# Second-layer work of two batches spread over four slots, and Gelu tiles in pairs, in a two-layer token tower

## The reference

```python
h = h + _L0_ffn_ref(_layernorm(h), ...)    # 8 heads, product keys, causal attention
h = h + _L1_attn_ref(_layernorm(h), Wq, Wk)   # q, k = x Wq^T, x Wk^T; softmax(q k^T / 8) @ x, no mask
h = h + _L1_ffn_ref(_layernorm(h), ...)    # experts, below

logits = tokens @ router_w.T; probs = softmax(logits)
rw, re = top_k(probs, 2); rw = rw / rw.sum(-1)
combine = zeros((N, 8)).at[arange(N)[:, None], re].set(rw)
out = tokens
for e in range(8):
    out = out + combine[:, e:e+1] * (gelu(tokens @ w1[e] + b1[e]) @ w2[e] + b2[e])
```

## Time and profile before

| | before |
|---|---|
| median of 3 runs | 3322.91 us (3321.53 to 3324.5) |
| the profiled execution's own time | 3329.95 us |
| its span | 3328.1 us |
| PE busy | 2803.7 us, 84% |
| VectorE busy | 2745.1 us, 82% |
| ScalarE busy | 2051.7 us, 62% |
| GpSimd busy | 2049.2 us, 62% |
| mean granted TensorE clock | 0.92 |

### The profile page before, as it was taken

How to read it: one execution, slowest core, us unless ns; L and a number is a source line. 1 busy time by engine, 2 the same in 40 slices (tenths; PEclk the granted TensorE clock), 3 DMA queues, 4 the chain that set the end, 5 groups by cost and what they waited for, 6 DMA issues and landing times. The chain is left out here.

```text
span 3328.1 us, 39343 instructions
## 1 busy us (share of the span) xinstructions
PE 2803.7 (84%) x9750; PEld 1333.8 (40%) x9750; DVE 2745.1 (82%) x10000; ACT 2051.7 (62%) x4514; POOL 2049.2 (62%) x2094
## 2 busy tenths in 40 slices
PE   4863466888989898989897989999988889899988
PEld 2431222343434343434344434344444434444433
DVE  8666987989898989897889998997989898966423
ACT  4222455676767676767686767676686767676422
POOL 4010577777777777777666777776657777776200
PEclk8975677999999999999898989999999899999989
DMA  1001122222222222222121222221212222221000
GB/s 43 26 10 49 34 65 63 64 64 61 67 64 65 63 64 65 63 64 63 49 67 41 70 61 70 56 73 50 66 47 62 65 65 63 64 63 49 20 0 4
DMA packets 85770, 179.92 MB, mean 54 GB/s; under 512 B 40193, under 2 KB 41251, under 8 KB 85542
## 3 DMA queue, kind: packets, MB, share of 16 engines
q0 software_dynamic: 66560, 135.40, 16.0%
q1 hardware_dynamic: 18982, 42.01, 4.0%
HBM read 176.22 MB, written 1.05 MB: 53 GB/s over the span
## 5 line engine op out<-in xcount | busy, mean ns | idle before, releaser
L1333 POOL DMA_INDIRECT mx_G<-in_kv_table,mx_slot_i x2048 | 1993.1, 973 | 815.4 <-issue 606.4
L1361 PE MATMUL mx_acc<-mx_W,mx_table 128*128 128x512 f32 x2048 | 1114.1, 626 | 0.3 <-ACT mx_kvT L1562 0.3
L1719 DVE SCALAR_TENSOR_TENSOR mx_W<-mx_D,mx_W 128x512 f32<-128x512 f32 x1024 | 697.2, 681 | 260.6 <-ACT mx_W L1555 258.5
L1623 ACT ACTIVATE mx_GT<-mx_G,mx_slot_w 128x128 f32<-128x128 f32 x2048 | 759.0, 494 | 208.9 <-DMA mx_G<-in_kv_table,mx_slot_i 208.5
L1555 ACT ACTIVATE mx_W<-mx_D 128x512 f32<-128x512 f32 x1024 | 606.9, 593 | 165.1 <-PE mx_D L1351 160.7
L1361 PEld LDWEIGHTS mx_acc<-mx_W,mx_table 128*128 128x128 f32 x2048 | 412.6, 203 | 193.8 <-issue 114.8
L1351 PE MATMUL mx_D<-mx_U,mx_pick_b 96*128 96x512 bf16 x1024 | 412.3, 403 | 60.0 <-DVE mx_W L1719 58.4
L1579 ACT ACTIVATE mx_PT<-mx_area 128x512 f32<-128x512 f32 x480 | 246.8, 514 | 284.9 <-PE mx_area L1411 147.0
L1373 PE MATMUL mx_O<-mx_PT,mx_KVs 128*65 128x512 f32 (+3 forms) x768 | 312.7, 489 | 16.9 <-ACT mx_OT L1571 8.7
L1387 PE MATMUL mx_area<-mx_KTa,mx_QTa 64*128 64x512 f32 (+3 forms) x384 | 179.3, 548 | 156.7 <-DVE mx_mx_part L1954 126.2
L1936 DVE TENSOR_REDUCE mx_KVs<-mx_GT 128x128 f32<-128x2048 f32 x128 | 291.8, 2280 | 6.9 <-ACT mx_GT L1623 6.7
(11 more groups left out here) (380 smaller groups left out, 4370.6 us busy)
## 6 DMA issues: line engine op xcount, KB each, us to landing
mx_table<-in_kv_dense SPq DMA_DIRECT2D x64, 512.0 KB, 3.7
mx_G<-in_kv_table,mx_slot_i POOLq DMA_INDIRECT x2048
tz_table<-in_c_dft SPq DMA_DIRECT2D x1, 2048.0 KB
tz_table<-in_c_idft SPq DMA_DIRECT2D x8, 256.0 KB, 2.6
out_h<-mx_xc SPq DMA_DIRECT2D x4, 256.0 KB, 3.8
mx_G<-in_c_pick SPq DMA_DIRECT2D x1, 528.0 KB
st_h<-in_tok_W,em_ids POOLq DMA_INDIRECT x32, 2.5
st_keys<-in_pk_keys SPq DMA_DIRECT2D x1, 512.0 KB, 3.9
```

The costliest lines, as they stand in the source:

```text
L1333: pool.indirect_dma_start(G[g % RING][:, r, :], None, a["kv_table"], bass.IndirectOffsetOnAxis(slot_i[n % 2][:, k, r:r + 1], 0))\
L1361: pe.matmul(acc[:, :], table[:, tile, :], W[c % TILE_RING][:, :], start=(tile == 0), stop=(tile == TILES - 1)).then_inc(applied, 1)
L1623: last = act.activation(GT[:, :, i], G[g % RING][:, i, :], ACT.Copy, scale=slot_w[n % 2][:, k, i:i + 1])
L1719: dve.scalar_tensor_tensor(W[c % TILE_RING][:, :], D_ps[c % 3][:, :], 0.0, W[c % TILE_RING][:, :], ALU.is_ge, ALU.mult).then_inc(w_done, 1)
```

## The change

Batches 0 and 1 get a fifth slot, which is slot s = 0 of the batch behind them: L1T tiles 0 to 7 stay in s = 2 and tiles 8 to 15 go to s = 3, at their positions 8 to 15; the second `l1y`, the norm, the router and the routing go from s = 2 to s = 3 at their positions; the experts, the final addition go from s = 3 to s = 4. Batches 2 and 3 stay as they were (`route_slot` is 2 there). For all batches the first norm goes from positions 11, 13, 14 to 22, 24, 25, and HID tiles come in pairs, at k = 1 and k = 3 of their half, none at k = 0 and 2. No operation is added or taken away in the source.

```diff
@@ area_uses @@
-    if p < 16 and 0 <= t - 6 < 4 * B:
-        b, s = divmod(t - 6, 4)
-        if s == 1:
-            return (("L1S", b, 0, p),)
-        if s == 2:
-            return (("L1T", b, 0, p),)
-        if s == 3:
-            return (("HID", b, p // 8, p % 8) if p % 8 < 4 else ("MY", b, 0, p // 8 * 4 + p % 8 - 4),)
+    if p < 16:
+        for b, s in cycle_of(t):
+            if s == 1:
+                return (("L1S", b, 0, p),)
+            if s == (2 if p < 8 else route_slot(b)):
+                return (("L1T", b, 0, p),)
+            if s == route_slot(b) + 1:
+                return expert_uses(b, p)
     return ()
+
+def route_slot(b):
+    return 3 if b < B - 2 else 2
+
+def expert_uses(b, p):
+    half, k = divmod(p, 8)
+    if k in (1, 3):
+        return (("HID", b, half, k - 1), ("HID", b, half, k))
+    return (("MY", b, 0, 4 * half + k - 4),) if k >= 4 else ()
+
+def cycle_of(t):
+    b, s = divmod(t - 6, 4)
+    stages = [(b - 1, 4)] if s == 0 and 0 < b <= B and route_slot(b - 1) == 3 else []
+    return stages + ([(b, s)] if 0 <= b < B else [])
@@ extra_uses @@
         if s == 2:
-            uses += [(10, ("l1y", b, 0)), (19, ("l1y", b, 1)), (28, ("l2x", b, 0)), (29, ("l2x", b, 1)), (32, ("l2r", b))]
+            uses += [(10, ("l1y", b, 0))]
+        if s == route_slot(b):
+            uses += [(19, ("l1y", b, 1)), (28, ("l2x", b, 0)), (29, ("l2x", b, 1)), (32, ("l2r", b))]
@@ tensor: the loop over q @@
-                elif uses:
-                    fill_area(uses[0])
+                else:
+                    for use in uses:
+                        fill_area(use)
@@ scalar: F @@
-                if (s, p) in ((0, 13), (2, 24)):
-                    act.wait_ge(ln_var, 2 * b + s // 2 + 1)
+                if p == 24 and s in (0, route_slot(b)):
+                    act.wait_ge(ln_var, 2 * b + (s > 0) + 1)
...
-                if (s, p) == (2, 35):
+                if (s, p) == (route_slot(b), 35):
@@ vector: F @@
-                n = s // 2
-                if (s, p) == (0, 11) and b:
+                n = int(s > 0)
+                if (s, p) == (0, 22) and b:
                     dve.wait_ge(out_stored, 16 * b)
-                if (s, p) in ((0, 11), (2, 22)):
+                if p == 22 and s in (0, route_slot(b)):
...
-                if (s, p) in ((0, 14), (2, 25)):
+                if p == 25 and s in (0, route_slot(b)):
...
-                if (s, p) == (2, 33):
+                if (s, p) == (route_slot(b), 33):
...
-                if (s, p) == (3, 17):
+                if (s, p) == (route_slot(b) + 1, 17):
@@ scalar and vector: the loop over q @@
-                if 0 <= t - 6 < 4 * B:
-                    F((t - 6) // 4, (t - 6) % 4, p)
+                for b, s in cycle_of(t):
+                    F(b, s, p)
```

More of the change, by code:

```diff
@@ L1536, in _ @@
                 uses = area_uses(q)
-                if len(uses) == 2:
+                if uses and uses[0][0] == "S":
                     if q >= LAST:
@@ L2008, in F @@
                        .then_inc(route_in, 1)
-                if (s, p) == (2, 37):
+                if (s, p) == (route_slot(b), 37):
                     dve.wait_ge(route_out, b + 1)
@@ L2016, in F @@
                     chain.wait()
-                if (s, p) == (2, 41):
+                if (s, p) == (route_slot(b), 41):
                     for t in range(NB):
@@ L2020, in F @@
                     chain.wait()
-                if (s, p) == (2, 45):
+                if (s, p) == (route_slot(b), 45):
                     chain.mark(dve.tensor_copy(pif[:, :, :], pi[:, :, :]))
```

## The result

The changed kernel takes 3301.3 us (median of 4 runs, 3299.56 to 3304.84) against 3322.2 for the kernel before beside it: 20.9 us less, ratio 0.9933 with a 95% interval of 0.992 to 0.9945. The forecast was 3315.0, with a range of 3304 to 3326, so the direction was right and the gain 2.6 times the forecast, outside the range. The profiled execution has a span of 3299.1 us.

What follows compares the result with a forecast made beforehand. The bound changes inside a slot: ScalarE's table loads and PE in the experts' positions 0 to 15, VectorE in 16 to 39, PE in 40 to 63. Loads -20.4, norms +12, rest +0.5: 3322.9 - 7.9 = 3315.0 us, range 3304 to 3326.

Steps and rivals of the forecast that it cites:

- spreading: Four slots in place of three for batches 0 and 1; forecast +0.5 us, the difference of light slots.
- Part 1: HID tiles in pairs, experts' first sixteen positions: sixteen table loads fewer, 62.2 to 52.0 us; -20.4 us in the sum.
- the four pieces: Experts' sixteen positions in fours, forecast 15.4, 11.0, 12.6 and 13.0 us.
- The rival in which PE takes the gain: First 16 positions of slots 10 and 14 take 57 us instead of 52, leaving 3325; chance 0.19, whole or in part.
- The dearer switch: A drain makes each ScalarE table switch cost more than its load; experts' stretch 50.5 us, total 3312; chance 0.02.
- Part 2: First norm of slots 6, 10, 14: 0.7 us gained at position 11, 4.0 charged at 22; norms +12 in the sum.
- the 7 us that I had named as a sign of being wrong: The prediction counted itself wrong if the moved norm cost over 7 us.
- the slower rival: Norm's round trip and store wait at 22 to 25 cost up to 11.7 us each, not 4.0; chance 0.09.
- Part 3: L1T, norm, routing and experts over four slots at unchanged positions, costs moving along; slots 8 to 10 sum to 536.3 us.
- These two terms of the sum: Slot 8's positions 8 to 15 at 20.2 us (light) and slot 9's, with L1T, at 27.5.
- The levelling rival: Light halves of slots 8 and 9 absorb work, moved norms cost 1 to 2 us: -16 to -18, 3306; chance 0.16.
- Its words on the gathers: The levelling rival's claim that gathers catch up; no separate size given.

Runs made afterwards that it cites:

- norm_only: Kernel before with only the first norm moved to positions 22, 24, 25 from 11, 13, 14: 3332.9 against 3325.0 us, ratio 1.0019 (norm_only_c, chip without stalls).
- together_c: Changed kernel with all 16 L1T tiles and both head sums in slot s = 2 again: 3310.4 us, ratio 0.9954 to the kernel before.

## Why the prediction missed

Part by part, for the slots with dense tiles, with the medians where a kernel had only that part, and with the widths of the slots that the part is in (9 and 13 for the pairs; 6, 10 and 14 for the norm; 6, 8 to 10 and 12 to 14 for the whole):

| term | forecast | by medians | by widths |
|---|---|---|---|
| pairs | -20.4 | -23.1 (3304.07 - 3327.13) | -21.4 |
| norm | +12 | +7.8 (3332.85 - 3325.01) | +6.7 |
| spreading, by difference | +0.5 | -5.6 | -6.3 |
| whole | -7.9 | -20.9 | -21.0 |

By the intervals of the ratios each difference of medians is uncertain by some 3 to 6 us.

**Part 1, right, slightly low.** Sixteen loads, 20 Gelu loads to 12, and nearly all of their time reaches the end. Three of the four pieces were forecast within 1.2 us; the fourth came out at 11.2 us for 13.0, with PE at full clock. The rival in which PE takes the gain asked for PE to keep a clock near 0.8; it has 0.97 over the sixteen positions, weighed from the four rows, and the 0.81 of slot 9 was already 0.92 in slot 13. The dearer switch is out as well: between two loads and two Gelus of the changed kernel there is again no time for a drain.

```profile
1913.69 1.28 ACT L1602 ACT_TABLE_LOAD   x1
1914.98 1.27 ACT L1602 ACTIVATE mx_PT<-mx_area 128x512 f32<-128x512 f32 x2
1916.27 1.28 ACT L1578 ACT_TABLE_LOAD   x1
1917.56 0.60 ACT L1578 ACTIVATE mx_W<-mx_D 128x512 f32<-128x512 f32 x1
```

From 1913.69 to 1917.56 are 3.87 us: two loads 2.57, two Gelus 1.27, 0.03 left.

**Part 2, the term that was mis-sized downwards at its old place.** "Taking it away there is worth 0.7 us" compared slot 10 with the mean of slots 3 to 5. It is 4.0 by the same slot with and without the norm. The new place was mis-sized too, 4.0 for 6.5 (7.4 and 8.6 in slots 14 and 6, past the 7 us that I had named as a sign of being wrong). The errors cancel in part in norm_only, and the net is +7.8 for +12. The store was hidden and the root's round trip at 24 cost nothing of its own (VectorE is idle 0.6 us in all in positions 16 to 39 of slot 10), so the slower rival did not come.

**Part 3, the step that failed.** "Every item keeps its position, so its neighbours are alike and the cost goes with it." Same position is not the same neighbours. Sixteen L1T tiles in a row keep PE full for 52.5 us; eight leave a half behind them that runs at 17.4 and not 20.2 us, and eight behind an empty half take 24.2 and 24.7 and not 27.5. These two terms of the sum are off by 6.1 us in the first triple and 5.6 in the second, 11.7 of the 13.0 us by which the whole forecast was off; the other errors nearly cancel. What an engine is behind when a stretch begins is part of that stretch's width, and a mean over other slots does not have it. The levelling rival (0.16, 3306) came nearest: light halves did get shorter, and the moved norms cost 1.7 to 2.6 us net in norm_only_c, where it had 1 to 2. The measured 3301.3 lies below its 3306 too. Its words on the gathers were not tested.

The range was too narrow at its lower end for this reason: its -18 took the tables fully free and the norms at 1 to 2, but levelling at nothing. The -6 of the spreading is the split of L1T: undoing the split alone (together_c) lengthens slots 8, 9, 12 and 13 by 8.4 us, so nothing is left to explain by the norm and the routing that no longer follow a full half. These are single profiled executions; by the times the same run has +4.2 by the medians and 0.2% by the ratios, with intervals that overlap. Why PE's clock was 0.81 in slot 9 and 0.92 in slot 13 stays open.

## What to carry to other kernels

In a pipeline whose engines are only a few steps apart, price a moved piece by its length, by what stands directly before it and by what it puts on the other engines, not by the busy share of the stretch: the same norm cost 3 to 6 us in one piece beside ten idle microseconds of its engine, in large part because its root's table loads held up a copy that PE waited for; in steps of 0.7 us with the root elsewhere it cost almost nothing. Put equal heavy items on every second position rather than in a row: here it gained another 7 us in slots 3 to 15. And before using a mean of similar stretches as the price of a stretch without something, look for the same stretch with and without it, or allow the difference between the similar ones as the error of each.

## What was not expected of the hardware

- Chips on which instructions stall at issue, VectorE's at a spacing of 0.71 us, ScalarE's and PE's too: the kernel before takes 3884 to 3926 us there, 17 to 18% more, the granted clock is 0.86 to 0.87 for 0.92, and a gain of 0.7% vanishes, one of 1.7% shrinks to 0.3%. The part behind the last activation of W is not slower there (219.3 us).
- PE's clock differs with other engines' work: with eight table loads fewer on ScalarE the mean granted clock over the experts' sixteen positions was 0.97 in the changed kernel and 1.00 with the pairs alone. Before it was 0.81 in slot 9 and 0.92 in slot 13, with the same loads, so the loads are not all of it.
- A switch of ScalarE's function set costs its load, 1.283 us, and hardly more. The Trainium skill (ScalarE: Activation LUTs, section What ACT_TABLE_LOAD costs) adds a drain of about 1.38 us; the two stretches of 3.82 and 3.87 us, before and after, have no room for it, and the measurement decides.
